# A delta rule stage with a new order of its step on every engine, on one core

## What is computed

```
q = (h @ q_w).reshape(bsz, seq, H, DK)
k = (h @ k_w).reshape(bsz, seq, H, DK)
v = (h @ v_w).reshape(bsz, seq, H, DV)
q = q / (jnp.linalg.norm(q, axis=-1, keepdims=True) + EPS)
k = k / (jnp.linalg.norm(k, axis=-1, keepdims=True) + EPS)
alpha = jax.nn.sigmoid(h @ alpha_w + alpha_b).reshape(bsz, seq, H, DK)
beta = jax.nn.sigmoid(h @ beta_w + beta_b)
def step(s, inp):
    qt, kt, vt, at, bt = inp
    s = s * at[..., None]
    u = jnp.einsum('bhd,bhdv->bhv', kt, s)
    s = s + bt[..., None, None] * (kt[..., None] * (vt - u)[..., None, :])
    out = jnp.einsum('bhdv,bhd->bhv', s, qt)
    return (s, out)
```

## Time and profile before

| | |
|---|---|
| time, median of 3 runs | 5489.76 us (5489.14 to 5496.58) |
| span of the profiled execution, first to last instruction | 5145.8 us |
| what lies around the span (difference to the median) | 344.0 us |
| ScalarE's copy into kd (L3049), first and last of 65 | 1485.0 and 3860.7 us |
| from one step to the next, mean, (3860.7 - 1485.0) / 64 | 37.1 us |
| the same, shortest and longest of twelve neighbouring steps | 35.2 and 41.0 us |

### The profile page before, as it was taken

One profiled execution on the slowest core, in us unless ns is written; L12 is line 12 of the kernel. 1 busy time (PEld: TensorE's weight loads), 2 busy tenths in 40 slices (PEclk: granted clock), 3 DMA queues, 4 the chain that ended last, 5 costly groups with the idle time before them and its releaser, 6 DMA issues. The chain is left out here.

```text
span 5145.8 us, 181702 instructions
## 1 busy us (share of the span) xinstructions
PE 3922.1 (76%) x73332; PEld 3131.2 (61%) x73332; DVE 2953.6 (57%) x8172; ACT 1773.9 (34%) x4061; POOL 2629.7 (51%) x3000
## 2 busy tenths in 40 slices
PE   4779973674068888888888888888886679588695
PEld 2534443664047676766677676767674479477595
DVE  5832267755556665656556566656555645488723
ACT  3732231442023333333333333333333134211163
POOL 2310016514546666666666666666664242477644
PEclk8989986886579999999999999999998889799797
DMA  0030003664000000000000000000000056200154
GB/s 22 2 138 0 0 3 95 190 181 121 23 15 14 11 14 11 14 11 14 11 11 14 11 14 11 14 11 14 11 14 8 18 208 229 87 1 1 61 187 125
DMA packets 129703, 249.33 MB, mean 48 GB/s; under 512 B 24672, under 2 KB 60656, under 8 KB 127344
## 3 DMA queue, kind: packets, MB, share of 16 engines
q1 hardware_dynamic: 98224, 178.93, 11.0%
q0 software_dynamic: 16384, 33.59, 2.2%
q10 hardware_dynamic: 14400, 26.22, 1.4%
HBM read 178.89 MB, written 59.77 MB: 46 GB/s over the span
## 5 line engine op out<-in xcount | busy, mean ns | idle before, releaser
L2597 POOL TENSOR_TENSOR e_kd<-e_kd,e_tail 128x512 f32<-128x512 f32 x325 | 368.9, 1135 | 587.2 <-PE psum L2709 586.7
L2739 PE MATMUL psum<-e_T,e_N 64*64 64x32 f32 x10400 | 402.3, 228 | 71.3 <-remote 34.8
L2739 PEld LDWEIGHTS psum<-e_T,e_N 64*64 64x64 f32 x10400 | 363.3, 141 | 100.7 <-issue 99.7
L2709 PE MATMUL psum<-e_kd,e_k 64*64 64x64 f32 x10400 | 396.7, 228 | 28.6 <-DVE e_AT L3127 28.4
L729 POOL DMA_INDIRECT m_back<-m_rows_out,m_idx x256 | 253.3, 990 | 295.8 <-DVEq L1169 121.5
L2709 PEld LDWEIGHTS psum<-e_kd,e_k 64*64 64x64 f32 x10400 | 361.2, 143 | 37.3 <-issue 37.1
L3133 DVE COPY e_Z<-psum 64x256 f32<-64x256 f32 x325 | 135.8, 418 | 386.0 <-PE psum L2739 384.2
L3022 ACT ACTIVATE e_T<-psum 128x256 f32<-128x256 f32 x325 | 125.9, 387 | 631.1 <-PE psum L2760 631.1
L723 POOL DMA_INDIRECT rows_in<-xn,m_idx x256 | 256.0, 1000 | 145.5 <-issue 76.2
L840 PE MATMUL psum<-m_rowsT,m_w 128*128 128x128 f32 x2304 | 317.3, 297 | 3.0 <-DVE m_h L1145 2.3
L2760 PE MATMUL psum<-e_Z,e_TT 64*64 64x32 f32 x8320 | 297.6, 222 | 26.7 <-DVE e_Z L3133 21.2
(11 more groups left out here) (464 smaller groups left out, 10744.4 us busy)
## 6 DMA issues: line engine op xcount, KB each, us to landing
m_w<-in_m_w SPq DMA_DIRECT2D x88, 516.0 KB, 5.7
m_w<-in_m_w SPq DMA_DIRECT2D x224, 129.0 KB
m_rows<-rows_in SPq DMA_DIRECT2D x100, 256.0 KB, 3.8
m_rows_out<-m_out ACTq DMA_DIRECT2D x100, 256.0 KB, 2.1
m_w<-in_m_w SPq DMA_DIRECT2D x88, 259.0 KB, 3.6
e_w<-in_e_w SPq DMA_DIRECT2D x66, 321.0 KB, 3.0
rows_in<-xn SPq DMA_DIRECT2D x6, 2048.0 KB, 23.4
m_wd<-in_m_wd SPq DMA_DIRECT2D x3, 2048.0 KB, 8.1
```

Source lines behind the costliest of these rows:

```text
L2597: return g.tensor_tensor(both_odd(dst[:], m), both_odd(src[:], m), gate.unsqueeze(1).broadcast_to((P, 2, nb, m)), ALU.mult)
L2709: r = pe.matmul(c.psum[half(h), G_, chunk(u)], keys[half(h), chunk(u)], both_odd(gated[half(h), :, chunk(u)], 1 << l), start=True, stop=True)
L2739: r = pe.matmul(c.psum[half(1 - h), Z_, u * HC:(u + 1) * HC], N[half(h), l - 1, chunk(u)], even(T[half(h), chunk(u)], 1 << l), start=True, ...
```

## The change

Nothing is computed differently, except that the square of q and k and their copies are now two instructions each. What moves:

- **TensorE.** `project_q` moves from behind `t_step(1)` to between `solve(0)` and the state product of block 0; `project_k` to between `solve(1)` and the state product of block 1. `state_and_output` is split in `state` and `from_inputs`, and `from_state` in itself and `outputs_from_state`, so that products for the outputs can stand behind others. `t_step(1)` goes behind `state(1)`, `t_step(2)` behind `solve(2)`, `z_and_gram(3)` behind the products of block 2, `t_step(3)` behind `solve(3)`.
- **ScalarE.** `squares` becomes `raw_queries` (square and copy of q, as soon as q is there) and `key_squares` with `raw_keys`. `t_copy(5)` goes ahead of the copy of AT, `u_copy(1)` ahead of the Z copy of level 1.
- **VectorE.** The outputs are added half by half: the 4 instructions of head 0 with the two `rq` copies stand at the very end of the loop body, those of head 1 behind `state(0)`. `first_t`, the transpose of T, goes behind the AT copy of level 0.
- **GpSimd.** `hidden` is copied one piece further ahead, at the end of the loop body. `gated_queries` goes ahead of `carry(4)`.

The diff, cut to its core:

```diff
@@ gpsimd @@
             with g.Fori(0, LAST + 1) as i:
...
                 carry(1)
                 g.sem_inc(kn_free, 1)
-                g.wait_ge(hs_free, 1)
-                g.sem_clear(hs_free)
-                hidden(i + 1)
                 g.tensor_copy(owp[:], ow[:, bass.ds(((i + LAST - 1) % LAST) // B, 1), :].rearrange("p o d -> p (o d)"))
                 carry(2)
                 carry(3)
                 roots()
+                gated_queries()
                 carry(4)
-                gated_queries()
                 tail_products()
...
                 g.sem_inc(kd_free, 1)
+                g.wait_ge(hs_free, 1)
+                g.sem_clear(hs_free)
+                hidden(i + 2)
@@ tensor, step() @@
                 solve(0)
-                state_and_output(0)
+                pe.wait_ge(q_free, 1)
+                pe.sem_clear(q_free)
+                project_q()
+                state(0)
+                from_inputs(0)
                 from_state(1)
                 z_and_gram(1)
+                outputs_from_state(1)
                 solve(1)
+                pe.wait_ge(ks_free, 1)
+                pe.sem_clear(ks_free)
+                project_k()
+                state(1)
                 t_step(1)
-                pe.wait_ge(out_free, 1)
-                pe.sem_clear(out_free)
-                project_q()
-                state_and_output(1)
-                project_k()
+                from_inputs(1)
                 from_state(2)
+                outputs_from_state(2)
                 z_and_gram(2)
                 square_sums()
-                t_step(2)
                 project_gate(0)
                 solve(2)
+                t_step(2)
+                state(2)
+                from_inputs(2)
                 z_and_gram(3)
-                state_and_output(2)
+                from_state(3)
                 project_gate(1)
-                from_state(3)
+                outputs_from_state(3)
+                solve(3)
                 t_step(3)
-                solve(3)
+                from_inputs(3)
+                key_norms()
                 z_and_gram(4)
-                key_norms()
-                state_and_output(3)
                 project_v()
                 t_step(4)
@@ scalar @@
                 t_copy(0)
+                raw_queries()
+                u_copy()
                 z_copy()
-                t_copy(1)
-                u_copy()
-                squares()
+                key_squares()
                 a.wait_ge(kn_free, 1)
                 a.sem_clear(kn_free)
-                raw_qk()
+                raw_keys()
+                t_copy(1)
                 z_copy()
+                u_copy()
                 t_copy(2)
@@ vector @@
             with v.Fori(0, LAST + 1) as i:
                 ch.reset()
                 rest = masked(0, gr0_ps)
...
                 rest()
-                v.wait_ge(tx_ps, 1)
-                v.sem_clear(tx_ps)
-                v.tensor_copy(flat(TX), c.ps[Z_][:, TB * CH:]).then_inc(tx_ready, 1)
-                v.wait_ge(rs_ready, 1)
-                v.sem_clear(rs_ready)
-                v.wait_ge(out_ps, 1)
-                v.sem_clear(out_ps)
-                ch.link(v.tensor_copy(rq[0][:], rq[1][:]))
-                ch.link(v.tensor_copy(rq[1][:], rq[2][:]))
-                accumulate(i, 0, (0, 1))
+                first_t()
+                cross_t_copy()
                 masked(1, gr_fwd)()
                 state(0)
-                ch.link(accumulate(i, 0, (2, 3)))
-                accumulate(i, 1, (0, 1))
+                accumulate(i, 1).then_inc(ks_free, 1)
                 residual(1)
...
                 state(1)
-                rest()
+                seen = masked(3, gr_fwd)
                 transposed(1)
+                sums_in()
+                residual(2)
                 z_copy()
-                masked(3, gr_fwd)()
-                residual(2)
-                sums_in()
+                seen()
+                state(2)
                 transposed(2)
+                norms()
+                residual(3)
                 z_copy()
-                norms()
-                state(2)
-                masked(4, gr_fwd)()
-                residual(3)
                 key_scales(0)
                 key_scales(1).then_inc(rk_ready, 1)
+                masked(4, gr_fwd)()
+                transposed(3)
+                scaled_keys()
                 z_copy()
-                transposed(3)
-                normed_keys()
                 masked(5, gr_fwd)()
+                beta_keys()
...
                 transposed(5)
+                v.wait_ge(rs_ready, 1)
+                v.sem_clear(rs_ready)
+                v.wait_ge(out_ps, 1)
+                v.sem_clear(out_ps)
+                accumulate(i + 1, 0).then_inc(q_free, 1)
+                next_norms()
```

More of the change, by code:

```diff
@@ L2642, in _ @@
             g.sem_inc(kdh_done, 1)
-            g.sem_inc(rs_ready, 1)
             hidden(0)
@@ L2980, in _ @@
                     step()
-            for token in (nx_ready, t_ready, tt_ready, ket_ready, kdh_done, kd_ready):
+            for token in (nx_ready, t_ready, tt_ready, ket_ready, kdh_done, kd_ready, q_free, hs_ready):
                 pe.wait_ge(token, 1)
@@ L3160, in residual, with first_t, cross_t_copy, next_norms @@
                 v.tensor_tensor(own, own, c.ps[H_][:, 0:P], ALU.add).then_inc(r_ready, 1)
-            def accumulate(i, h, ts):
-                for t in ts:
+            def first_t():
+                v.transpose(c.ps[T_], TT0[:]).then_inc(t0_ready, 1)
+            def cross_t_copy():
+                v.wait_ge(tx_ps, 1)
+                v.sem_clear(tx_ps)
+                v.tensor_copy(flat(TX), c.ps[Z_][:, TB * CH:]).then_inc(tx_ready, 1)
+            def next_norms():
+                ch.link(v.tensor_copy(rq[0][:], rq[1][:]))
+                ch.link(v.tensor_copy(rq[1][:], rq[2][:]))
+            def accumulate(i, h):
+                for t in range(TB):
                     acc = c.xn[:, bass.ds(((i + B - 2) % B) * TB + t, 1), :].rearrange("p o d -> p (o d)")
```

84 lines of the change are left out of this document (45 added, 39 removed).

## The result

The changed kernel takes 5541.4 us (median of 4 runs, 5531.04 to 5575.14), the kernel before beside it 5489.45. The ratio is 1.010, 95% interval 1.007 to 1.013: slower by 52 us, where 5457 was forecast. Beside later experiments it was timed again, 5199.64 against 5155.34 us, ratio 1.008 (1.005 to 1.010).

What follows compares the result with a forecast made beforehand. TensorE was taken to set the pace, with about 13% of holes. Holes -0.2 and clock -0.3 make -0.5 us a step, over 65 steps -33 us: 5457 us against 5489.76, range 5305 to 5535.

Steps and rivals of the forecast that it cites:

- The full-clock step: A stage step at 2.4 GHz, 35.3 us before: holes that go (-4.7) and come (+4.75) nearly balance; -0.2 us taken.
- the 1.1 us a step for `square_sums`: TensorE's hole ahead of square_sums (0.74 us and a few late ones) goes, as less ScalarE work lies behind k.
- the 0.95 at `solve(3)`: New TensorE wait: residual(3) stands behind VectorE's norms, which meets GpSimd's gated_queries and gating of carry(4); +0.95 us a step.
- The seam: Step boundary on VectorE: accumulate and two rq copies now precede the first masked copy; gram(1) at 5.7 instead of 3.55, +2.15 us.
- The blocked copies: The two rq copies at the step's end wait for GpSimd instructions to end: near 0.8 us instead of 0.171.
- The walk without the block: Same sum with rq copies not held up by GpSimd: L3123 at 2.75 us, gram(1) at 4.4, +0.85 us.
- Rival (a): The rq copies are not held up by GpSimd and most low clock goes: -2.4 us a step, 5334 us; chance 0.28.
- the forecast case: Rq copies held up, -0.5 us a step, 5457 us; own range 5415 to 5520, chance 0.50.
- The clock: TensorE's falls to 1.2 GHz, costing about 1.2 us of the mean step: -0.3 taken, bounds -1.2 and +1.3.
- rival (b): The 2.6 us hole at the step's start drops the clock in every step: +1.1 us a step, 5562 us; chance 0.14.
- The place where the unrolled body begins anew: Where TensorE's unrolled body restarts, costing some 4 us in 4 of the steps (41.0 us); claimed to be left alone.
- The span: Forecast span 5145.8 - 33 = 5113 us, with 344.0 us around it added to give 5457 us.

Runs made afterwards that it cites:

- the runs with fillers: Changed kernel with 12, then 7 further products that nobody reads in TensorE's hole between cross_t and gram(1): 1.005 and 1.001 of the kernel before.
- moved copies: Changed kernel with only the two rq copies moved from the end of VectorE's step to behind state(1): 0.979 and 0.983 of the kernel before.

## Why the prediction was wrong

The forecast was 33 us faster; the kernel became 52 us slower. By terms of the prediction's sum:

**The full-clock step: near, its sign open.** Forecast -0.2 us. The fit of step length against time at low clock (without the four steps where the unrolled body begins anew) gives 35.77 us before and 35.53 after at none: -0.24; the shortest steps are 35.0 to 35.3 and 34.3 to 34.7 us. The mean of the steps without low clock went the other way, 35.67 to 35.87. The terms behind it erred in both directions. U's hole is gone, so is most of the one ahead of `from_state(3)` (9.5 us of waits for S are left of 69.2), and half of those ahead of the levels' products (30.1 us of 64.7). Of the 1.1 us a step for `square_sums` 0.3 came (36.9 us of idle time there instead of 55.9): with ScalarE out of the way TensorE paused in issue. `norms` was not blocked (L3217, 0.132 us in the median), so the 0.95 at `solve(3)` never came. The seam cost 1.9 us in the median, 5.4 against 3.55, instead of 2.15.

**The blocked copies: right**, with the row that was asked for (0.8 us; L3123, now L3145, "some 4 us behind a step's start": 3.7 in the median). The walk without the block was right as well: with the copies through PSUM L3145 begins at 2.7 and `gram(1)` at 4.5 us (2.75 and 4.4 in the prediction). Rival (a)'s price was not: it put the kernel without the block at 5334 us, 123 below the forecast case; taking the block away brought 93 us and left the kernel at 0.990 of the one before, and low clock at 235 us (348 with the block), where most of it was to go.

**The clock: the step that failed.** "I take 0.3 off; bounds -1.2 and +1.3." It rose: 113 us more of low clock (297 and 184) at about 0.4 us each are +46 us, +0.7 a step, a full microsecond from my value and inside the bounds, half of what rival (b) set for the clock. That is one of the signs of being wrong that the prediction named (the clock's share moving by more than half a microsecond). The upper bound did not follow from its own row either: 38.5 - 35.3 - 1.2 is 2.0 and not 1.3, and for the reason given for less (a part falls where TensorE does not set the pace) there was no row. I weighed that one hole was exchanged for another and called the rest open, though in the kernel before the clock fell behind a hole of 0.74 us in half of the steps, and the new one is 2 us. The argument against, "products behind gram(1) come close together", was about what stands behind the hole; the runs with fillers show that the hole itself brings the fall.

**The place where the unrolled body begins anew: left out.** "Which the change leaves alone" was wrong: the four steps there went from 40.6 to 43.3 us in the mean (41.0 to 43.8 in the rows), +11 us. The seam lies next to it: with the seam put back these steps take 41.3 us.

Together: -0.24 + 0.7 + 0.17 = +0.63 us a step, +41 us; measured +39.5 in the stage and +52 in the time. (The first term and the price of low clock come out of one fit, so that they add up is no proof of either; the runs with fillers and moved copies are.) The range was closed at 5535 because rival (b) had 0.14; with the length of the new hole set against that of the old one it deserved far more.

**The span.** I took the median minus the span as time around it. It was the difference between two chips; the difference that I added to it is not touched by that.

## What to carry to other kernels

A small VectorE copy within SBUF beside steady GpSimd work can cost what is left of GpSimd's instruction, as it did here: put it where VectorE waits anyway, or give it an operand in PSUM. Don't end a loop body with an instruction that is waited for if other work can stand there; here work that nobody waited for hid the loop's turn of 0.70 us. And when a change trades many short holes for one longer, price the clock by what a hole of that size does in the trace at hand, before the sum of idle time.

## What the runs showed of the hardware

- In this stage the clock fell to 1.2 GHz behind a hole of 0.74 us in half of the steps (33 of 64, before; 17 with that hole filled) and behind one of 2 us in more than a third (24 of 64, after); each us at low clock costs about 0.4 us. Seven useless 128x128 products in the second hole won 0.9%.
- A VectorE copy of 8 elements, 0.17 us alone, takes 0.83 us in the median beside GpSimd, and 0.156 with one operand in PSUM.
- Behind a dense group of small products, the thin ones of `square_sums` paused TensorE by over 0.8 us in a third of the steps, up to 2.2 us, and the pause ended 1.2 to 1.6 us behind the arrival of a 16 KB block of the instruction queue. That the block is the cause is not shown.
- Two kinds of chip, 330 us apart on the same program outside this stage (5155 and 5489 us), with the same ratios to within 0.5%.
